# Edge attention on one core: exponentials in a PSUM bank of their own, and the edge units' small fills spread over slots

## The reference

```
q, k, v = (xp @ Wq + bq), (xp @ Wk + bk), (xp @ Wv + bv)      # 8 heads of 16
att = einsum('ehd,ehd->eh', q[dst], k[src]) / 4               # clipped to +-50, nan to 0
ex = exp(att - segment_max(att, dst)[dst])
alpha = ex / segment_sum(ex, dst)[dst]
aggr = segment_sum(v[src] * alpha, dst)
x = x + aggr @ Wo + bo
x = x + gelu(layernorm(x) @ W1 + b1) @ W2 + b2
```

## Time and profile before

| | |
|---|---|
| median of 3 runs | 3679.43 us (3673.75 to 3686.6) |
| the profiled execution | 3681.54 us, of which span 3679.6 us |
| clock granted to PE, mean | 0.904 of full speed |
| edge stage, layer 0 | POOL's gathers from 289.7 to 2002.3 us |
| edge stage, layer 1 | POOL's gathers from 2047.3 to 3635.3 us |
| behind the last gather | 44 us |

### The profile page before, as it was taken

How to read it: one execution, slowest core, us unless ns; L and a number is a source line. 1 busy time by engine, 2 the same in 40 slices (tenths; PEclk the granted TensorE clock), 3 DMA queues, 4 the chain that set the end, 5 groups by cost and what they waited for, 6 DMA issues and landing times.

```text
span 3679.6 us, 74225 instructions
## 1 busy us (share of the span) xinstructions
PE 3094.9 (84%) x25656; PEld 2455.6 (67%) x25656; DVE 2917.6 (79%) x6187; ACT 1812.1 (49%) x4404; POOL 2567.7 (70%) x2470
## 2 busy tenths in 40 slices
PE   3993589898898998998997588888888888989896
PEld 3762467677777776776775466766677676767675
DVE  8986578888888898888886468777887777878886
ACT  1331135454555554555564345555555555655565
POOL 1006777777777777777775577777777777777774
PEclk7675679999999999999999799999999999999997
DMA  3006345555555555555553455555565555555552
GB/s 86 23 26 187 112 140 164 157 165 156 161 175 160 174 161 157 172 153 162 158 174 107 134 160 173 171 175 165 166 181 171 170 171 173 172 173 165 166 180 71
DMA packets 426827, 558.32 MB, mean 152 GB/s; under 512 B 78430, under 2 KB 345020, under 8 KB 426256
## 3 DMA queue, kind: packets, MB, share of 16 engines
q0 software_dynamic: 117504, 321.02, 29.8%
q1 hardware_dynamic: 301442, 225.28, 20.1%
q10 hardware_dynamic: 7506, 7.20, 0.6%
HBM read 527.79 MB, written 25.44 MB: 150 GB/s over the span
## 4 chain that ended last, share of the span: by engine, by line
POOL 34%; PE 25%; DVE 21%; issue 13%; ACT 4%; DMA 1%; DVEq 1%; POOLq 0%; SPq 0%
POOL kv_ring L1969 26%; POOL arena L1969 8%; PE psum L958 4%; DVE scratch L1680 3%; DVE scratch L1704 3%; PE psum L1032 3%; DVE att L1689 3%; PE psum L1015 2%; PE psum L1069 2%; PE psum L1048 2%; PE psum L999 2%; DVE work L1384 2%; DVE kv_ring L1401 2%; PE psum L834 1%; DVE arena L1731 1%
## 5 line engine op out<-in xcount | busy, mean ns | idle before, releaser
L1969 POOL DMA_INDIRECT kv_ring<-kv_table,src_idx x1840 | 1922.9, 1045 | 634.3 <-issue 557.3
L1234 ACT ACTIVATE scratch<-psum 128x512 f32<-128x512 f32 (+1 forms) x1228 | 698.4, 569 | 501.8 <-PE psum L968 338.6
L1969 POOL DMA_INDIRECT arena<-kv_table,src_idx x608 | 626.4, 1030 | 189.5 <-issue 184.6
L958 PE MATMUL psum<-arena 128*128 128x256 f32 x2156 | 628.0, 411 | 111.7 <-ACT scratch L1234 111.4
L958 PEld LDWEIGHTS psum<-arena 128*128 128x128 f32 x2156 | 378.1, 195 | 236.0 <-ACT scratch L1234 144.5
L1689 DVE TENSOR_REDUCE att<-scratch 128x64 f32<-128x1024 f32 (+1 forms) x460 | 535.4, 1164 | 0.2
L1680 DVE TENSOR_TENSOR scratch<-psum,kv_ring 128x1024 f32<-128x1024 f32 x230 | 280.6, 1220 | 285.7 <-DMA kv_ring<-kv_table,src_idx 228.1
L1245 ACT COPY arena<-psum 128x512 f32<-128x512 f32 x616 | 326.4, 531 | 297.0 <-PE psum L958 287.7
L1269 ACT ACTIVATE scratch<-att 128x64 f32<-128x64 f32 (+1 forms) x460 | 117.2, 255 | 685.9 <-DVE att L1695 681.6
L999 PEld LDWEIGHTS psum<-q_win,scratch 64*128 64x128 f32 x4896 | 326.0, 203 | 177.3 <-issue 172.4
L999 PE MATMUL psum<-q_win,scratch 64*128 64x128 f32 x4896 | 387.4, 302 | 67.2 <-DVE scratch L1680 59.4
(11 more groups left out here) (252 smaller groups left out, 4681.1 us busy)
## 6 DMA issues: line engine op xcount, KB each, us to landing
arena<-kv_table SPq DMA_DIRECT2D x154, 896.0 KB
kv_ring<-kv_table,src_idx POOLq DMA_INDIRECT x1840
q_win<-q_table SPq DMA_DIRECT2D x612, 32.0 KB
work<-kv_table SPq DMA_DIRECT2D x98, 128.0 KB
q_win<-q_table SPq DMA_DIRECT2D x154, 64.0 KB
arena<-kv_table,src_idx POOLq DMA_INDIRECT x608
work<-q_table SPq DMA_DIRECT2D x98, 64.0 KB
kv_table<-work SPq DMA_DIRECT2D x49, 128.0 KB
```

Source lines behind the costliest of these rows:

```text
L958: mm = e.matmul(to[:, t % 2 * 2 * D:(t % 2 + 1) * 2 * D], hot_source[:, t * P:(t + 1) * P], source_rows[m % 2][:, t, :], start=True, stop= ...
L1234: e.activation(to[:, at:at + width], apart[k % FILL_BANKS][:, 0:width], ACT.Relu, bias=1.0, scale=-1.0).then_inc(apart_read, 1)
L1969: e.indirect_dma_start(kv[m % RING_KV][:, t, :], None, kv_table[l], bass.IndirectOffsetOnAxis(ap=src_idx[:, c * T + t:c * T + t + 1], axis ...
```

## The change

ACT takes the exponentials of a unit twice: first into 64 columns of PSUM bank 5, which nothing else uses then, and then into `msg` as before. DVE's message product reads them from the bank. The fills keep two banks. `Layer.fills` gives each fill a range of slots and puts it into the emptiest of them; the six slots above hold 2, 3, 2, 3, 3, 1 fills, never more than 3. `source` and `rows` fills start up to three slots earlier, `turn` and `hot` up to one. Fills evicted behind the exponentials are 179 single ones. On PE the third fill of a slot goes ahead of the node steps, and any left over goes between them. On ACT the GELU of a node tile is cut in halves with evictions between. PE's sum of messages also waits for the second exponentials.

```
-FILL_BANKS = 3
+FILL_BANKS = 2
...
+        def place(first, last, of):
+            first, last = max(first, -1), max(last, -1)
+            slot = min(range(first, last + 1), key=lambda at: (len(fills[at]), -at))
+            fills[slot].append(of)
+            return slot
...
+                done = [place(2 * v - 10 + h, 2 * v - 8 + h, ("source", v, h)) for h in range(2)]
+                at = 0
+                for i in range(4):
+                    at = place(max(at, done[i // 2] + 1, 2 * v - 8 + i), max(at, done[i // 2] + 1, 2 * v - 7 + i), ("rows", v, i))
...
+                    at = place(max(at, 2 * v - 5), 2 * v - 4, ("turn", v, h))
...
+                    at = place(max(at, 2 * u), 2 * u + 1, ("hot", u, h))
...
+        def exps(l, u):
+            ts = LAYERS[l].tiles_of(u)
+            return psum[:, 5, 0:ts * H].rearrange("p (t h) -> p t h", h=H)
...
-        def one_hots_made(e, k, since):
-
-            if since < k + FILL_BANKS:
+        def one_hots_made(e, k):
+
+            assert k < issued[0]
+            if issued[0] <= k + FILL_BANKS:
                 e.wait_ge(apart_read, k + 1)
...
             e.wait_ge(msg_ready, n + 1)
+            e.wait_ge(exp_ready, 2 * n + 2)
...
             e.wait_ge(score_ready, n + 1)
+            if n >= 1:
+                e.wait_ge(msg_ready, n)
+            e.activation(exps(l, u), att[:, n % 2, 0:ts], ACT.Exp).then_inc(exp_ready, 1)
...
-            e.wait_ge(exp_ready, n + 1)
+            e.wait_ge(exp_ready, 2 * n + 1)
             e.tensor_tensor(msg[n % 2][:, 0:ts, 0:D].rearrange("p t (h d) -> p t h d", d=HD),
                             values.rearrange("p t (h d) -> p t h d", d=HD),
-                            msg[n % 2][:, 0:ts, D:MW].unsqueeze(3).to_broadcast([P, ts, H, HD]), ALU.mult
+                            exps(l, u).unsqueeze(3).to_broadcast([P, ts, H, HD]), ALU.mult
```

On PE, in `tensor_edges`, and on ACT, in `scalar_edges`:

```
                     for h in range(2):
-                        for fill_of in fills[h:h + 1]:
-                            tensor_fill(e, l, *fill_of)
+                        next_fill(e, l, fills)
...
-                    for fill_of in fills[2:]:
-                        tensor_fill(e, l, *fill_of)
+                    next_fill(e, l, fills)
                     for j, k in at(slots, slot):
                         node_tensor(e, l, j, k, True)
+                        if k in BANKED:
+                            next_fill(e, l, fills)
...
+                        if k == GELU:
+                            gelu_half(e, l, j, 0)
+                            next_scalar_fill(e, l, fills)
+                            gelu_half(e, l, j, 1)
+                            next_scalar_fill(e, l, fills)
```

More of the change, by code:

```diff
@@ L162, in fills @@
     def fills(self):
[L165 to L172, removed]
+        fills = {slot: [] for slot in range(-1, 2 * self.nu + 2)}
+        def place(first, last, of):
[3 more added lines that the diff above has]
+            return slot
+        for u in range(2):
+            for h in range(self.parts_of(u)):
+                fills[-1].append(("turn", u, h))
+        for v in range(self.nu + 4):
+            if self.is_block(v):
+                done = [place(2 * v - 10 + h, 2 * v - 8 + h, ("source", v, h)) for h in range(2)]
+                at = 0
+                for i in range(4):
+                    at = place(max(at, done[i // 2] + 1, 2 * v - 8 + i), max(at, done[i // 2] + 1, 2 * v - 7 + i), ("rows", v, i))
+            if 2 <= v < self.nu:
+                at = 0
+                for h in range(self.parts_of(v)):
+                    at = place(max(at, 2 * v - 5), 2 * v - 4, ("turn", v, h))
+            u = v - 3
+            if 0 <= u < self.nu:
+                at = 0
+                for h in range(self.parts_of(u)):
+                    at = place(max(at, 2 * u), 2 * u + 1, ("hot", u, h))
         return fills
@@ L597, in fill @@
             return FILL_AT[l, what, u, h]
[L599 to L603, removed]
+        issued = [0]
         def unit(l, u):
             return LAYERS[l].unit0 + u
+        def exps(l, u):
+            ts = LAYERS[l].tiles_of(u)
+            return psum[:, 5, 0:ts * H].rearrange("p (t h) -> p t h", h=H)
         def chunk(l, c):
@@ L980, in tensor_fill @@
             n = unit(l, u)
+            assert FILL_ORDER[issued[0]] == (l, what, u, h)
+            issued[0] += 1
             if what == "turn":
@@ L988, in tensor_fill, with next_fill @@
                 gather_rows(e, n, h)
+        def next_fill(e, l, fills):
+            for fill_of in itertools.islice(fills, 1):
+                tensor_fill(e, l, *fill_of)
         def spread_chunk(e, l, u):
             n = unit(l, u)
-            one_hots_made(e, fill(n, "turn", 0), fills_before(l, 2 * u - 2))
+            one_hots_made(e, fill(n, "turn", 0))
             e.wait_ge(q_in[n % QUERIES], 16 * q_loads[n])
@@ L1338, in node_scalar @@
             elif k == GELU:
[L1339 to L1344, removed]
+                for h in range(2):
+                    gelu_half(e, l, j, h)
             elif k == 24:
@@ L1350, in node_scalar, with next_scalar_fill @@
                              bias=cols[:, l + 1, 3:4]).then_inc(next_ready, 1)
+        def next_scalar_fill(e, l, fills):
+            for fill_of in itertools.islice(fills, 1):
+                scalar_fill(e, l, *fill_of)
         def scalar_edges(e):
```

40 lines of the change are left out of this document (29 added, 11 removed).

## The result

The changed kernel takes 3565.83 us (median of 4, 3554.17 to 3570.75) against 3683.01 us before (median of 4): ratio 0.9678, 95% interval 0.9656 to 0.9701, so 3.2% or 117 us faster. The prediction was 3562 us, with a range of 3476 to 3640. The profiled execution took 3564.98 us, of which span 3563.0. Line 1969 is now 2026 (gathers), 1680 is 1737 (products), 1704 is 1761 (messages), 1032 and 999 are 1059 and 1025 (spreads), 1234 and 1245 are 1267 and 1278 (evictions), 1269 is 1302 (into PSUM); the fills' products at 946, 958, 968 and 976 are at 965, 977, 987 and 995.

The account below looks back on a forecast made before the run. POOL was taken to bound most stretches, PE and DVE 521 to 1840 us. 3681.5 - 105.6 (exponentials in PSUM) + 3.7 (PSUM product) - 15.5 (fills) = 3564.1, less 2.1 above the median: 3562 us, range 3476 to 3640.

Parts of the forecast that it names:

- The bound: POOL paces where products wait for gathers, at 1.25 us per indirect DMA; PE and DVE pace 521 to 1840 us.
- The relief of POOL: Message products with two SBUF inputs lengthen gathers, 236 us excess; nine tenths goes, mean gather 1041 ns to 955 or less.
- part 1: Exponentials in PSUM, relief of POOL's gathers counted by stretch: 105.6 us gained, 3.7 us cost.
- product in PSUM: DVE's message product reading PSUM takes 1220 ns against 1212: 8 ns x 460, 3.7 us lost.
- The least of three: Gain per stretch is the least of nine tenths of the excess, waits for gathers, and length less PE's busy time over 0.911.
- The fourth rival: The interference stays or is not the cause: 3668 us, or 3680 without the gain from the fills; chance 0.07.
- PE's 91.1%: PE's busy share from 521 to 1840 us, taken as the most the present order of work gets out of it.
- part 2: Fills spread over slots on two banks: a quarter of the 61.9 us DVE waits on layer 0's spreads, 15.5 us gained.
- The rival of the missing bank: PE waits behind ACT at 179 fills evicted behind the exponentials: up to 265 us, 3741 us at 1 us each; chance 0.08.
- One sign of being wrong: ACT or PE waits at fills grown by more than 100 us would point to the banks.
- Costs put at nothing: ACT's 460 more exponentials, 117 us, taken as hidden; earlier source-row reads priced at nothing; GELU halves delay ACT's chain by one or two evictions.
- The first rival: PE freed past its 91%, POOL the bound throughout, so relief counts everywhere: 203 us, 3476 us; chance 0.15.

Follow-up runs that it names:

- f: The kernel before with only the first 4 of 8 gathers of each chunk issued, the other tiles constant: 3478.75 us, ratio 0.9447.
- d: The changed kernel with both sets of exponentials still made, but the message product reading those in SBUF: 3686.76 us, ratio 1.0005 to the kernel before.
- a: The kernel before with exponentials read from PSUM, old fills in their old slots, two fill banks: 3716.29 us, ratio 1.0076.
- b: The changed kernel's fills on two banks, but one set of exponentials, made and read in SBUF: 3691.82 us, ratio 1.0010 to the kernel before.
- c: The kernel before with two fill banks in place of three and nothing else: 3738.77 us, ratio 1.0145.
- g: The changed kernel with only the first 4 of 8 gathers of each chunk issued: 3478.12 us, ratio 0.9446 to the kernel before.
- h: The changed kernel with ACT's exponentials into `msg` put behind the third eviction of the slot: 3575.67 us, ratio 0.9705 to the kernel before.
- j: The changed kernel with up to three evictions ahead of the exponentials: 5960.45 us, ratio 1.0439, on another chip where the kernel before took 5710.01 us.
- e: The changed kernel's fills on three banks, one set of exponentials read in SBUF, half of the gathers left out: 3371.70 us, ratio 0.9157 to the kernel before.

## Why the prediction was right, and where it was not

**The bound.** Right: gathers back to back at 1.25 us, lengthened by the message product, and PE and DVE at their own pace from 521 to 1840 us. f confirms the second to 2 us. That this was the only limit there was wrong (below).

**The relief of POOL.** The mechanism is shown by d against the changed kernel. Size: gathers at 957 and 956 ns, where 955 or less was written. Layer 0's gathers end 47 us earlier (30 to 45 written) and layer 1's take 79 us less (80 written).

**The sum by stretch.** Forecast, part 1 and the fills together, against measured:

| stretch | forecast gain | measured |
|---|---|---|
| 1 to 21 (305 to 521) | 10.0 | 14.2 |
| to 201 (521 to 1840) | 4.8 + 15.5 (fills) | 23.3 |
| to 227 (1840 to 2003) | 11.0 | 13.7 |
| to 401 (2047 to 3230) | 64.8 | 58.1 |
| to 460 (3230 to 3636) | 15.0 | 11.8 |
| product in PSUM | -3.7 | not there: 1208 ns against 1212 |
| all | 117.4 | 116.6 in span |

The stretches gained 121.1 us together, and 4.6 were lost outside them (a later start and a longer change of layers, less a shorter tail). No stretch is off by more than 7 us. Three slips in the working are small. The least of three for 1840 to 2003 us was nine tenths of the excess, 10.2, and not 11.0. ACT's fullest stretch is 56% busy (226.29 of 406 us), not 53%. The fourth rival without the gain from the fills comes to 3683 us (3681.5 + 3.7 - 2), not 3680. To take the least of three limits in each (excess, waits, PE at its ceiling) was right; PE's 91.1% was a rough ceiling (92.1% in 502 to 1797, but 88.4% in 2017 to 3133, where waits for gathers are left).

**The step that failed: that the parts add up.** Part 1 was priced at 105.6 - 3.7 = 102 us and part 2 at 15.5, each by itself. By itself part 1, with the bank that it takes, costs 28 us (a: 0.0076 x 3684.85), and part 2 gives nothing measurable (b: +0.1%, -0.1 to +0.3). Two things were mis-read. First, in the long stretch of layer 0 I took PE and DVE for the only limit, because the products waited 4.8 us for gathers. But POOL hardly waited either, and where neither of two waits for the other both are at their limit: 1316 and 1315.6 us. Second, the bank. I set it off against the smoother order in one term, "a gain of a quarter", with a rival of 0.08 for a costly one. Apart, they are +53 us (c) and -47 us (b against c), and in the long stretch +52.3 us (c) and -59.3 (b against c). The net, 22.5 us by own pace there (f against g), is near the 15.5 written, but in layer 1 the net is 16.0 us the other way. So that the sum came out within 1 us is in part luck: 4.8 + 15.5 stands against 23.3 in the long stretch, although there neither term would have come by itself.

**The rival of the missing bank.** It named the right resource and the wrong place. I had put it at the fills behind the exponentials. In c, PE's new waits stand at the `turn` and `hot` fills that follow the `rows` fills closely, +140 and +158 us; single fills behind the exponentials are what the changed kernel has, and h, which moved one instruction at that place, found nothing. Whether the exponentials hold the bank in the changed kernel was to be seen in j, and isn't. One sign of being wrong did show: PE's waits for ACT at the fills grew by more than 100 us, 297.7 to 403.3. The time came out all the same, so this sign didn't tell the rival from the forecast.

**Costs put at nothing.** The second exponentials: ACT's busy time rose by 84 us, h finds no cost in their place, and b and d, without and with them, take the same time. But there POOL sets the pace; what they cost at the own pace of PE, ACT and DVE is not shown. The halves of GELU and the earlier reading of source rows: no wait of the changed kernel's points to them; none of them was tried alone.

**The first rival** (POOL the bound throughout, 3476 us) would have needed about 1319 - 95 = 1224 us in the long stretch. No kernel here comes to that: the changed kernel's own pace is 1293.5 (g), and with a third bank and one set of exponentials it is 1275.2 (e). All eight banks are in use: with the exponentials in one, a third fill bank would have to come from the three of the node steps and edge sums. That was not tried.

## What to carry to other kernels

Read the waits in both directions before calling a stretch bound by one engine: where the consumer doesn't wait for the producer and the producer doesn't wait for the consumer, there are two limits of the same height, and a change that lowers only one shows nothing. Such parts have to be tried together before either is dropped. If an engine that issues DMAs shows two lengths for one instruction, lay the long ones against the other engines' instructions; here the place of one small operand was worth 3.3% with the new fills, and 0.7% with the old ones on two banks. And when a buffer is given up, look at which instructions follow each other through it, and part them first.

## What was not expected of the hardware

- The message product takes no longer from PSUM, 1208 against 1212 ns, though each exponential is read 16 times there. The fixed cost by the Trainium skill ("VectorE: DVE Perf Modes", section on the TRN2 errata) does not show in this instruction any more than in the products of the earlier trace rows.
- ACT's exponentials take less time into PSUM: 104.5 us for 460, 227 ns each, against 255 into SBUF before. In the changed kernel itself the second ones, into SBUF (line 1305), take 243 ns each. These follow the first ones without a wait, so a kernel's own pair gives 16 ns for the place, and the two kernels give 28. The Trainium skill, "ScalarE: Activation LUTs", section "Step-by-step: what each stage is for", calls PSUM the faster destination; these rows agree.

```profile
L1302 ACT ACTIVATE psum<-att 128x64 f32<-128x64 f32 (+1 forms) x460 | 104.5, 227 | 301.1 <-DVE att L1752 294.1
...
L1305 ACT ACTIVATE scratch<-att 128x64 f32<-128x64 f32 x306 | 74.8, 244 | 0.0
```

- A gather is not slowed, it is held. Before, 327 gathers start while a message product has 0.2 us or more to go, and 315 of them end 0.81 to 0.83 us behind the product's end, whether 0.3 or 1.1 us of it was left. The two long ones of the earlier trace rows show it: the product at 601.61 ends at 602.83 and the gather at 603.64, the product at 322.17 ends at 323.39 and the gather at 324.20. In the changed kernel the gathers beside the message product take 0.946 us (median) wherever they start.
- Only POOL paid. Of the kernel before's 306 message products of 1024 columns, 219 started inside a running gather and took 1212 ns on average; the other 87 took 1212 too. The rule of the Trainium skill, "SBUF — State Buffer", section "Who interferes with whom", that whoever issues second is held, is borne out for POOL by the times above, and not for DVE by any run here.
